# Plain transposes of stacks and maxima, and an order planned in stretches by twelve policies

## The reference

```python
x = L0(x, ctx)   # cross attention, 20 heads of 8, + x
x = L1(x, ctx)   # norm, self attention, + x; norm, cross attention, + x; norm, feed-forward, + x
x = L2(x, ctx)   # cross attention with 8 heads of 20 over 508 keys, plus a second path over
                 # the last 4 context rows: attention of 96 rows over x, then over 4 keys
x = L3(x, ctx)   # as L1
# each attention: softmax(q @ k.T * dh ** -0.5) @ v, then @ Wo + bo
# feed-forward: a, g = split(h @ w1 + b1); out = (a * gelu(g)) @ w2 + b2, inner width 640
```

## Time and profile before

| | us |
|---|---|
| median of 3 runs | 925.65 (924.31 to 927.06) |
| the profiled execution | 921.37 |
| its span, first to last instruction | 919.6 |
| TensorE busy | 869.9 (95%) |
| VectorE busy | 691.2 (75%) |
| ScalarE busy | 654.0 (71%) |
| mean granted clock of TensorE, share of full | 0.976 |

### The profile page before, as it was taken

One profiled execution on the slowest core, in us unless ns is written; L12 is line 12 of the kernel. 1 busy time (PEld: TensorE's weight loads), 2 busy tenths in 40 slices (PEclk: granted clock), 3 DMA queues, 4 the chain that ended last, 5 costly groups with the idle time before them and its releaser, 6 DMA issues.

```text
span 919.6 us, 19851 instructions
## 1 busy us (share of the span) xinstructions
PE 869.9 (95%) x7796; PEld 592.3 (64%) x7796; DVE 691.2 (75%) x1653; ACT 654.0 (71%) x1416; POOL 56.6 (6%) x98
## 2 busy tenths in 40 slices
PE   8999999999999989999999999899899999999986
PEld 6666655666666656666677776556566666666665
DVE  4988788878888876777776675666777888779763
ACT  8778776877777877686777566457668687868571
POOL 2000000000001000100000000100000000000010
PEclk9999999999999999999999899869999999999999
DMA  4611221111111111010000200001111211111200
GB/s 107 184 42 36 64 56 32 26 28 25 28 38 35 36 33 27 19 36 18 13 1 2 76 2 2 23 2 39 62 25 29 47 36 35 25 35 25 49 1 15
DMA packets 26964, 32.45 MB, mean 35 GB/s; under 512 B 9333, under 2 KB 17913, under 8 KB 26873
## 3 DMA queue, kind: packets, MB, share of 16 engines
q1 hardware_dynamic: 26872, 31.19, 13.4%
HBM read 9.54 MB, written 0.66 MB: 11 GB/s over the span
## 4 chain that ended last, share of the span: by engine, by line
PE 75%; DVE 12%; ACT 10%; issue 2%; SPq 0%; DMA 0%; POOL 0%; DVEq 0%; ACTq 0%
PE pv_ps L1079 16%; PE bank_ps L1038 11%; PE bank_ps L1018 11%; DVE mx L1511 7%; ACT probs L1333 5%; PE bank_ps L1124 5%; PE bank_ps L1240 5%; PE bank_ps L999 5%; PE bank_ps L1000 4%; PE bank_ps L1104 4%; PE bank_ps L1052 4%; PE bank_ps L1205 3%; PE bank_ps L1251 3%; PE bank_ps L1192 2%; ACT hT_in L1394 1%
## 5 line engine op out<-in xcount | busy, mean ns | idle before, releaser
L1511 DVE TENSOR_REDUCE mx<-bank_ps 128x1 f32<-128x512 f32 (+3 forms) x720 | 451.4, 681 | 76.3 <-PE bank_ps L1038 74.3
L1333 ACT ACTIVATE probs<-bank_ps 128x512 f32<-128x512 f32 x736 | 380.2, 602 | 107.5 <-PE bank_ps L1018 105.6
L1079 PE MATMUL pv_ps<-probs,v_all 128*9 128x256 f32 (+2 forms) x2944 | 203.5, 380 | 5.8 <-ACT probs L1333 4.2
L1018 PE MATMUL bank_ps<-qT,ring 64*128 64x256 f32 x1280 | 173.7, 303 | 1.7 <-ACT probs L1333 0.2
L1018 PEld LDWEIGHTS bank_ps<-qT,ring 64*128 64x128 f32 x1280 | 133.1, 185 | 53.5 <-ACT probs L1333 13.7
L1038 PE MATMUL bank_ps<-ring,qT 64*128 64x512 f32 (+1 forms) x800 | 165.2, 400 | 2.0 <-DMA ring<-kdense 0.7
L1038 PEld LDWEIGHTS bank_ps<-ring,qT 64*128 64x128 f32 x800 | 86.0, 187 | 51.5 <-issue 26.3
L1079 PEld LDWEIGHTS pv_ps<-probs,v_all 128*9 128x9 f32 (+2 forms) x2944 | 57.8, 91 | 76.6 <-issue 23.6
L1384 ACT ACTIVATE kdense<-bank_ps 128x512 fp32r<-128x512 f32 (+2 forms) x116 | 58.3, 558 | 18.9 <-PE bank_ps L1124 18.7
L1311 ACT ACTIVATE ks<-bank_ps 128x320 fp32r<-128x320 f32 x80 | 35.7, 447 | 45.5 <-PE bank_ps L1000 23.1
L1535 DVE TENSOR_TENSOR qT<-bank_ps,qT 128x256 fp32r<-128x256 f32 (+1 forms) x108 | 47.0, 435 | 24.2 <-PE bank_ps L1052 23.9
(11 more groups left out here) (186 smaller groups left out, 1002.3 us busy)
## 6 DMA issues: line engine op xcount, KB each, us to landing
ring<-kdense SPq DMA_DIRECT2D x240, 64.0 KB, 2.0
ring<-kdense SPq DMA_DIRECT2D x160, 32.0 KB, 1.9
gate<-in_w_up SPq DMA_DIRECT2D x4, 640.0 KB, 4.1
wb<-in_w_blk SPq DMA_DIRECT2D x2, 960.0 KB, 5.4
wd<-in_w_down SPq DMA_DIRECT2D x2, 400.0 KB, 5.7
x<-in_x SPq DMA_DIRECT2D x4, 160.0 KB, 4.0
bias<-in_bias SPq DMA_DIRECT2D x1, 640.0 KB
out_rows<-x SPq DMA_DIRECT2D x4, 160.0 KB, 2.2
```

The costliest lines, as they stand in the source:

```text
L1018: mm = pe.matmul(bank[0:kr, i * a["nq"]:(i + 1) * a["nq"]], key_op(n, h)[:, c * P:c * P + kr], query_rows(u, b, h), start=True, stop=True)
L1079: mm = pe.matmul(pv_ps[32 * j:32 * j + a["dh"] + 1, 0:a["nq"]], v, probs[0:kr, s % N_P, i * a["nq"]:(i + 1) * a["nq"]], start=(c == 0), st ...
L1333: nc.scalar.activation(probs[0:kr, s % N_P, 0:w], bank[0:kr, 0:w], ACT.Exp, scale=float(a["dh"]) ** -0.5).then_inc(free, 1)
L1511: nc.vector.tensor_reduce(mx[b][0:rows, t, heads[0]:heads[-1] + 1:heads[-1] - heads[0] or 1], bank[0:rows, 0:a["hpm"] * a["nk"]].rearrange ...
```

## The change

Three sets of matmuls against `identr` become `pe.transpose` against `ident`, their inputs read as float32; `identr`, its semaphore, the activation that fills it and TensorE's wait for it go. `simulate()` gets `advance`, which carries a state forward by a given policy until a given time; every 25000 ns of the model twelve policies `WAYS` (horizon, weight of the readers' work, patience) are tried from the same state, and the steps of the one with the highest rate are kept. The readers' work is counted on its own (`drained`), and its weight is a part of the policy. `cost()` and what a step needs are as before.

```diff
-HORIZON = 12000
-PATIENCE = 800
+WAYS = [(h, o, p) for h in (8000, 12000, 16000) for o in (0.1, 0.2) for p in (500, 1000)]
+STRETCH = 25000
 OTHERS = 0.1
...
             for eng, ns in after:
                 t = self.clock[eng] = max(t + HANDOFF, self.clock[eng]) + ns
-                self.work += OTHERS * ns
+                self.drained += ns
...
-        def worth(self, choice):
+        def worth(self, choice, horizon, others):
 
             ahead = State(self)
             begin = max(self.lanes)
             ahead.take(choice)
-            while max(ahead.lanes) < begin + HORIZON:
+            while max(ahead.lanes) < begin + horizon:
                 left = ahead.choices()
                 if not left:
                     break
                 ahead.take(min(left, key=lambda c: c[0]))
-            return (ahead.work - self.work) / (max(ahead.lanes) - begin)
+            return (ahead.work - self.work + others * (ahead.drained - self.drained)) / (max(ahead.lanes) - begin)
+
+    def advance(state, horizon, others, patience, until):
+
+        while max(state.lanes) < until:
+            left = state.choices()
+            if not left:
+                return state
+            best = min(left, key=lambda c: c[0])
+            if facts(best[4])[1]:
+                first = {}
+                for c in sorted(left, key=lambda c: c[0]):
+                    if facts(c[4])[1] and c[0][0] <= best[0][0] + patience:
+                        first.setdefault(facts(c[4])[3], c)
+                if len(first) > 1:
+                    best = max(first.values(), key=lambda c: state.worth(c, horizon, others))
+            state.take(best)
+            state.steps.append((best[4], best[5]))
+        return state
 
     state, order, place = State(), [], {}
     while True:
-        left = state.choices()
-        if not left:
+        begin = max(state.lanes)
+        ends = [advance(State(state), *way, begin + STRETCH) for way in WAYS]
+        best = max(ends, key=lambda e: (e.work - state.work + OTHERS * (e.drained - state.drained)) / (max(e.lanes) - begin + 1))
+        if not best.steps:
             return order, place
...
-                                mm = pe.matmul(bank[:, k * a["nq"] + i * P:k * a["nq"] + i * P + rows], m, identr[0:rows, 0:rows],
-                                               start=True, stop=True)
+                                mm = pe.transpose(bank[:, k * a["nq"] + i * P:k * a["nq"] + i * P + rows], m.bitcast(F32), ident[0:rows, 0:rows])
...
-                        if (u, b, pr, gg) == (0, 0, 0, 0):
-                            pe.wait_ge(s_identr, 1)
...
-                                mm = pe.matmul(bank[:, k * SQ + t * P:k * SQ + t * P + kr],
-                                               ks[0:kr, t, g * of(u):(g + 1) * of(u), :].rearrange("p h s -> p (h s)"),
-                                               identr[0:kr, 0:kr], start=True, stop=True)
+                                mm = pe.transpose(bank[:, k * SQ + t * P:k * SQ + t * P + kr],
+                                                  ks[0:kr, t, g * of(u):(g + 1) * of(u), :].rearrange("p h s -> p (h s)").bitcast(F32),
+                                                  ident[0:kr, 0:kr])
...
-                act.wait_ge(s_ident, 16)
-                nc.scalar.activation(identr[:, :], ident[:, :], ACT.Copy).then_inc(s_identr, 1)
```

More of the change, by code:

```diff
@@ L527, in __init__ @@
             self.work = other.work if other else 0
+            self.drained = other.drained if other else 0
+            self.steps = list(other.steps) if other else []
         def at(self, step):
@@ L613, in worth @@
                 ahead.take(min(left, key=lambda c: c[0]))
-            return (ahead.work - self.work) / (max(ahead.lanes) - begin)
+            return (ahead.work - self.work + others * (ahead.drained - self.drained)) / (max(ahead.lanes) - begin)
[15 more added lines that the diff above has]
+        return state
     state, order, place = State(), [], {}
     while True:
-        left = state.choices()
-        if not left:
+        begin = max(state.lanes)
+        ends = [advance(State(state), *way, begin + STRETCH) for way in WAYS]
+        best = max(ends, key=lambda e: (e.work - state.work + OTHERS * (e.drained - state.drained)) / (max(e.lanes) - begin + 1))
+        if not best.steps:
             return order, place
[L621 to L629, removed]
+        for step, bank in best.steps:
+            order.append(step)
+            if bank is not None:
+                place[step] = bank
+        state = best
         state.past.update(state.done)
[L631 to L634, removed]
+        state.done, state.steps = {}, []
 SPARE = {"ctx_tr", "kv_proj", "k_tr", "q_proj", "q_tr", "qkv_proj", "o_nat", "o_tr", "o_proj", "h_tr", "ff_g", "ff_a",
@@ L1191, in _ @@
                             for i, (t, rows) in enumerate(q_tiles(u)):
-                                mm = pe.matmul(bank[:, k * nq + i * P:k * nq + i * P + rows],
-                                               query_stack(u, b)[0:rows, t, g * of(u):(g + 1) * of(u), :].rearrange("p h s -> p (h s)"),
-                                               identr[0:rows, 0:rows], start=True, stop=True)
+                                mm = pe.transpose(bank[:, k * nq + i * P:k * nq + i * P + rows],
+                                                  query_stack(u, b)[0:rows, t, g * of(u):(g + 1) * of(u), :].rearrange("p h s -> p (h s)").bitcast(F32),
+                                                  ident[0:rows, 0:rows])
                         mm.then_inc(full, 1)
```

2 lines of the change are left out of this document (removed).

## The result

| | before | changed |
|---|---|---|
| median, us | 926.09 (6 runs) | 890.87 (6 runs) |
| ratio | | 0.9641, interval 0.9583 to 0.9698 |
| the profiled execution, us | 921.37 | 890.55 |
| its span, us | 919.6 | 888.8 |
| mean granted clock in it | 0.976 | 0.994 |

The change is 3.6% faster.

The account below looks back on a forecast made before the run. TensorE's queue was taken as the bound. From the profiled 921.4 us, 4.5 for plain transposes and 8 for the order leave 908.9; 4.3 added back for the median gives 913, range 897 to 934 (8 in 10).

Parts of the forecast that it names:

- What bounds the kernel: TensorE's queue is the bound, busy 869.9 of 919.6 us (95%); the chain runs through it for 75%.
- Part 1: 912 fp32r matmuls against the rounded identity become plain transposes: 6.8 us off TensorE's queue, 4.5 us at the end.
- the signs that I named: For plain transposes: groups of ten take 1.28 us, pairs 0.41 us, weight loads 142 ns.
- Part 2: New order of TensorE's work saves one change of kind in ten, 11 us, 8 us reaching the end.
- the sign that I named for part 2: Line 1079's pieces become fewer and longer, and TensorE's busy time falls by more than 7 us.
- rival A: More of the span at half clock because plain transposes thin TensorE's counted work: 933 us, chance 0.10.
- rival D: Large gain: 22 us in place of 8 from the order, with fewer clock drops: 899 us, chance 0.12.
- The rule against part 1: Transpose-mode work doesn't count for TensorE's clock; some 100 us would stop keeping it up, so time comes out above.
- B: The order gives nothing on the chip and only the plain transposes' gain stays: 921 us, chance 0.17.
- C: The order loses: thin stretches make TensorE's idle time grow by a third, 17 us: 938 us, chance 0.13.

Follow-up runs that it names:

- the two kinds of fillers: Kernel before plus 77 fillers in ten places where TensorE idled: float32r matmuls 929.23 us (1.0021), plain transposes 921.35 us (0.9961).
- the bad single policy: Changed kernel planned by one policy alone (horizon 12 us, weight 0.2, patience 1 us), the longest plan: 939.14 us, 1.0178 to the kernel before.
- the worst of twelve: Changed kernel, but each stretch keeps the way with the lowest modelled rate: 941.95 us, 1.0158 to the kernel before.

## Why the prediction was wrong

**What bounds the kernel: right.** TensorE's queue is the bound in both traces, and the share of 75% with which I let a change of the queue reach the end was measured at 70%.

**Part 1, the price of a plain transpose: the term was mis-sized, though small.** I took 6.8 us from the queue. The lengths of pieces do shrink by that much: with the same order the three groups go from 150.3 to 143.6 busy us. But the length of a piece leaves out its entry, and there the plain form starts later; from start to start 0.7 us is left. The rows to price by were the distances from the piece ahead to the piece behind, not the pieces. Of the signs that I named, the weight loads came out (141 ns), tens take 1.25 to 1.31 us, 1.28 or close to it, but a pair of maxima still takes 0.44 us in 66 of 107 cases, not 0.41: I had priced it by one pair of line 1205 that was among the shorter ones. The end moved by 0.9 us in the new order and 1.7 in the old, not 4.5. The rounded identity's copy gave 0.2 of the up to 0.3 us that I allowed it.

**Part 2, by changes of kind: the wrong term.** I priced the order by one change in ten saved. Counted in the two plans, TensorE changes kind 760 times before, where I had taken 900, and 739 times after: 21 fewer, not 90, worth 2.5 us at my estimate of 0.12. Line 1079 has 235 pieces where it had 237, so the sign that I named for part 2, fewer and longer ones, is barely there. The order gave 15 us at the same clock (901.6 to 886.7). In the profiled executions 7.7 us of that is less idle time; the rest is denser work, above all between score matmuls: some 2000 steps from one of lines 1038 and 1018 to the next take 208.5 us before and 199.0 after, 6 us less when their 7 us less of half clock are taken off. That 8 us became 15 would still have left the time inside the range.

**The clock: the term that was left out, and the step that failed.** I knew from the earlier trace rows and the mean clock of 0.976 that 44 us ran at half clock, and that half clock costs up to half. I put a price on it in rival A alone, as a loss that could grow; that it could shrink stands in part 2 and in rival D in a clause each, and in the sum as nothing, with no reason given. Half-clock time fell from 54 us in the mean to 10, at 0.45 us each: 20 of the 35 us. So the gain of 35.6 us between the two means splits into 15 by the order at the same clock, 1 by the transposes and 20 by the clock. That these add up is no test, since the first two are what the third leaves; what tests the 0.45 are the four matched drops and the two kinds of fillers. By the run with the new order alone nearly all of the clock's part comes with the order, 54 to 13 us at half clock; plain transposes alone bring a part of it too, 54 to 30, and the two don't add up. With the clock's 20 us in the predicted sum it would have been 893; the two other terms, 16 us in place of 12.5, make up the rest.

**The rule against part 1.** The Trainium skill ("TensorE: Matmul & The Clock Gate", Part 4) has work in transpose mode not counting for the clock. Here more transposes in that mode went with less time at half clock in both pairs, 53.9 to 30.4 and 54.8 to 31.7 us. The measurements decide against the rule for float32 transposes in this kernel.

**The rivals.** A (the clock goes down) went the other way. One of its grounds was a wrong reading: that the stretch of 17 us holds 6.5 matmuls per us and the phase 7.9 doesn't show thin work, since at half clock the same work is spread over more time, 8.49 us for 5.54 in the matched stretch above. B (nothing from the order) and C (the order loses) are ruled out by the run with the order alone and, for C's mechanism, by the table: orders that the model ranks higher are faster. D had the right parts and the right sign, and stood at 899 with a chance of 0.12; even its time lies 8 us above the measured one, with 14 us more by the order and no price for the clock of its own.

**What stays open.** Which work lets the clock fall. Idle time goes with it: orders with 39 to 42 us idle spend 6 to 14 us at half clock, the old order with its 50 us 30 to 54, those with 58 and 61 us 46 and 35. But 77 matmuls put into idle places saved none. The drop of 17 us in phase 3 survived the fillers and plain transposes and went with every better order; a drop of 13.7 us stands there in the bad single policy, and none over 3.4 us in the worst of twelve. Why plain transposes in place of float32r ones save 23 us at half clock in the old order and 3 in the new isn't shown by any run.

## What to carry to other kernels

Before pricing an order, price the clock: if the runs of one program differ in granted clock, a line through time against half-clock time gives what a microsecond at half clock costs. A new order can win back that whole sum or add to it, so it belongs in the sum and in the range with a price of its own; filling single idle places did not win it back here. Price a changed matmul from the start of the piece ahead of it to the start of the piece behind it, since a shorter piece may only start later. Where a planner's model follows the chip at a constant distance, spend effort on the search over its policies, and compare plans by the model's end: taken to the same clock, it ranked all seven orders here as the chip did.

## What was not expected of the hardware

Half-clock time costs 0.45 us per us here, nearly the full half, though VectorE and ScalarE have work meanwhile. It varies between executions of one program on one chip by 34 us (34.7 to 68.9 in 23 executions), which at 0.45 makes 15 of the 17 us by which their times differ. In one and the same order a float32r 128 x 128 matmul that follows another full-array matmul starts 0.07 us after it in the mean of 47 and then takes 0.17 us to the next; a plain transpose starts after 0.20 us and goes on at 0.11. The shorter weight load, 141 ns against 197, shows in the piece's length and hardly in the queue.
